# Recurrent scan: where and when a segment's softmax and its local products are worked out

## The chip, the cores and the metric

The program runs on one core of a Trainium2 chip. Its time is the device time of one execution, from start to end, in microseconds; lower is better. Its four engines that matter here are TensorE (PE), VectorE (DVE), ScalarE (ACT) and GpSimd (POOL); SyncE (SP) issues the transfers. Each engine works through its own queue in order, and queues wait for one another by semaphores.

## The reference

Two blocks of a small model over x of 16 sequences, 512 positions, 128 features. The first block (attention in two forms, a mixture of experts) is not touched. The second is an attention with memory, over segments of 32 positions, 16 heads of 64, plus a linear layer in fp8 precision of the same normalized x:

```python
def step(carry, inp):                      # for each of 16 segments, every sequence and head
    mem, z = carry
    q_s, k_s, v_s, qn_s, kn_s = inp        # q, k with rotation by position; qn, kn without
    scores = jnp.einsum('bhnd,bhmd->bhnm', q_s, k_s) * SCALE
    scores = jnp.where(mask, scores, -jnp.inf)
    sdpa = jnp.einsum('bhnm,bhmd->bhnd', jax.nn.softmax(scores, axis=-1), v_s)
    sq = elu1(qn_s)
    mem_out = (sq @ mem) / (sq @ z + 1e-06)
    out = beta * mem_out + (1.0 - beta) * sdpa
    sk = elu1(kn_s)
    prev_v = (sk @ mem) / (sk @ z)
    mem = mem + sk.T @ (v_s - prev_v)
    z = z + sk.sum(axis=2)
    return ((mem, z), out)
```

and after the scan `out @ w_out`, added to x and to the fp8 layer's result with its bias.

## The kernel before

The second block is the function `scan`. Its queues are written out by hand: `turn` has one block with a loop over s for each engine, and in step s an engine does what stands there for pair s, s-1, s-2 and so on. A "pair" p is one segment and two heads: 16 segments of 8 pairs (`PAIRS`), so `PT` = 128 pairs, one a step, and a few steps more to empty the pipeline (133 in all). All 16 sequences are worked on together: as 4 groups g (`BG`) by 4 places f (`B1`), with the 32 positions of a segment for place f on partitions 32f to 32f+31.

For pair p the work goes: TensorE projects q and k, features on partitions, 512 columns (L2031), and v (L2037), into two banks of PSUM that take turns. ScalarE makes the parts of elu (L2180, L2182, L2185), VectorE finishes sigma of q (L2241), GpSimd sigma of k (`sigma_k`, L1990). VectorE starts the rotation of q or k (`rope`, L2234, L2235), GpSimd ends it (`rotate`, L1995, L1998). TensorE makes the scores one step later (L2071 the mask, L2076), VectorE takes the row maximum (L2279) and subtracts it (L2280), ScalarE exponentiates (L2202), VectorE transposes the result in 32x32 squares (L2300), sums it (L2302) and inverts the sum (L2303). TensorE multiplies with v (`local`, L2065), on the four diagonal 32x32 places of its array and into one bank; VectorE scales that by 1-beta and by the inverse sum (L2262). The parts recalled from memory (`recall`, L2047) are divided by VectorE (L2272, L2274 for k; L2291 to L2294 for q); GpSimd takes the k part from v (L2010) and adds the q part to the output of the heads (L2023). TensorE turns that (`turn_heads`, L2088), ScalarE copies it (L2214), TensorE adds it to the output projection, which sums over eight pairs in one bank (L2095); after the eighth ScalarE copies it (L2209), TensorE turns it (L2100), VectorE adds it to y (L2315). TensorE's memory update (`update`, L2055) is added by VectorE (L2251). Beside it one of the eight steps each normalizes, quantizes and loads the next segment (L1834 to L1893), and y gets its fp8 part and h with bias (L1867, L2309).

What sets the order around the change, in one step s:

- TensorE: project q, local (s-2), values, recall k (s-2), turn keys (s-1), mask and scores (s-1), project k, recall q (s-2), output projection (s-4), turn heads (s-3), update (s-4).
- ScalarE: q features, key copy (s-1), v copy, exponential (s-1), k features, heads' copy (s-3).
- VectorE: scale local (s-2), rope q, sigma q, recalled k (s-2), maximum and subtraction (s-1), recalled q (s-2), rope k, transposition and sum (s-1), additions to memory (s-4).
- GpSimd: rotate q, sigma k, new values (s-2), rotate k, addition of recalled parts (s-2).

Of the kernel before, what the change touches and what calls it, by code (L numbers as in the profile page):

```python
# [18 lines left out]
BF16 = mybir.dt.bfloat16  # L19
# [1739 lines left out]
def scan(nc, c, V, out, nseg):  # L1759
# [4 lines left out]
    with ExitStack() as ctx:  # L1764
# [3 lines left out]
        def sem(n):  # L1768
# [22 lines left out]
        oT, yT = sb("oT", [P, 2, S]), sb("yT", [P, S])  # L1791
# [4 lines left out]
                 "sx se pt pvd old kr_s qr_s kd ud qd od up mu ott otc oproj yt_c yt ydone stored0 stored1").split()  # L1796
# [11 lines left out]
        table = lambda name, q: V[name][:, q].unsqueeze(1).broadcast_to([P, S // SEG, SEG])  # L1808

# [13 lines left out]
        def load(sp, seg, j):  # L1823
            for f in range(B1):
                sp.dma_start(ht[32 * f:32 * f + 32, j % 2], h_seg[f, bass.ds(seg, 1)].rearrange("o i g d -> (o i) g d")).then_inc(G[f"h_in{j % 2}"], 16)

# [38 lines left out]
        def add_bias(pool, j):  # L1865
            wait_h(pool, j)
            pool.tensor_tensor(hb[:, j % 2], ht[:, j % 2], V["bias"][:].unsqueeze(1).broadcast_to([P, BG, D]), ALU.add).then_inc(G["hb_d"], 1)  # L1867
# [23 lines left out]
        def take_xq(act, bank, j, n):  # L1891
            wait(act, "xqt", n)
            act.copy(xqT[:, j % 2], ps[:, bank, 0:256].bitcast(BF16)).then_inc(G["xqt_c"], 1)  # L1893

        def prepare(seg):

            with nc.Block() as block:

                @block.sync
                def _(sp):  # L1900
                    load(sp, seg, 0)

# [26 lines left out]
        STEPS = PT + 5  # L1929
        inside = lambda p: 0 <= p < PT  # L1930
        starts = range(0, PT, PAIRS)

        def turn(seg, more):
# [13 lines left out]
            for s in range(STEPS):  # L1947
# [8 lines left out]
                if s - 12 in starts:  # L1956
                    user(("y", (s - 12) // PAIRS), "ydone", (s - 12) // PAIRS + 1)
# [9 lines left out]
            with nc.Block() as block:  # L1967

                @block.sync
                def _(sp):  # L1970
                    for j in sorted(readied)[:2]:
                        load(sp, seg + j, j)
                    for j in range(PER):
                        wait(sp, "ydone", j + 1)
                        for f in range(B1):
                            sp.dma_start(o_seg[f, bass.ds(seg + j, 1)].rearrange("o i g d -> (o i) g d"), y[32 * f:32 * f + 32, j % 2]).then_inc(G[f"stored{j % 2}"], 16)
                        if j + 3 in readied:
                            wait(sp, "xnn_d", j + 1)
                            wait(sp, "hb_d", j + 1)
                            load(sp, seg + j + 3, j + 3)  # L1980
                    for k in range(2):
                        wait(sp, f"stored{k}", 64 * (PER // 2))

                @block.gpsimd
                def _(pool):
# [14 lines left out]
                    for s in range(STEPS):  # L2000
# [4 lines left out]
                        p = s - 2  # L2005
                        if inside(p):
# [3 lines left out]
                            pool.tensor_tensor(new, new, t1[:, p % 2].rearrange("p (g h) d -> p g h d", h=2), ALU.subtract).then_inc(G["ud"], 1)  # L2010
                        if s < PT:
# [3 lines left out]
                        for j in at_step(s, 3):  # L2015
                            wait(pool, "ffn_c", j - 1)
                            add_bias(pool, j)
                        p = s - 2
                        if inside(p):
                            wait(pool, "qd", p + 1)  # L2020
                            wait(pool, "old", p + 1)
                            o = ol[:, p % 4].rearrange("p g h d -> p (g h d)")
                            pool.tensor_tensor(o, o, t2[:, p % 2].rearrange("p c d -> p (c d)"), ALU.add).then_inc(G["od"], 1)  # L2023

                @block.tensor
                def _(pe):
# [14 lines left out]
                    def recall(p, which, done):  # L2041
                        for g in range(BG):
                            for hh in range(2):
                                rows = slice(64 * hh, 64 * hh + 64)
                                for f in range(B1):
                                    at_ = g * P + 32 * f
                                    ins = pe.matmul(ps[32 * f:32 * f + 32, 2 + hh, g * VE:(g + 1) * VE],  # L2047
# [412 lines left out]
```

## Time and profile before

| | |
|---|---|
| median of 3 runs | 3117.67 us (3115.82 to 3118.49) |
| profiled execution | 3123.61 us, span 3121.8 us |
| PE busy | 2667.9 us, 85% of the span |
| DVE busy | 2507.4 us, 80% |
| ACT busy | 1875.7 us, 60% |
| POOL busy | 1760.6 us, 56% |

The page gives for each engine its busy time over the span, and cuts the span in 40 slices; the scan is what comes after about 1705 us, the last 18 of them, in which TensorE is busy for nine tenths and GpSimd for eight, against two before. The shares of the whole span therefore say little of the scan, and the rows below are taken from it, unless their line says otherwise. An idle time before an instruction is put down to the engine that released it; "issue" is idle time in which the engine waited for nothing that the profile shows.

### The profile page before, as it was taken

Reading aid. Unit: us, or ns where it says so; the run is one execution under the profiler, and the core shown is the slowest. Engines: PE = TensorE matmul, PEld = TensorE weight load, DVE = VectorE, ACT = ScalarE, POOL = GpSimd, SP = SyncE. Lnnn points to the kernel's source line nnn. Section 1 sums busy time; section 2 is a strip of 40 time slices with the busy share of each in tenths; the row PEclk is TensorE's granted clock in tenths of the full one; section 3 lists DMA queues with packets and bytes.
Section 4 is the critical chain, followed back from the end, with each engine's and each line's share of the span. In section 5 each row is a group of like instructions: output and inputs, shape, how many; then the busy total and the mean of one; then the engine's idle time right before and its main releaser. Section 6 shows DMA issues by size and latency. Waiting matters only on the chain. (4 is left out here: it accounts for less than half of the span.)

```text
span 3121.8 us, 129631 instructions
## 1 busy us (share of the span) xinstructions
PE 2667.9 (85%) x53553; PEld 1513.3 (48%) x53553; DVE 2507.4 (80%) x7598; ACT 1875.7 (60%) x3797; POOL 1760.6 (56%) x1988
## 2 busy tenths in 40 slices
PE   5787999999999999872331899999999999999998
PEld 2342333333333333372230666666666666666665
DVE  4678898999999999586606888888888888888886
ACT  5785999999999999630001555555445555455543
POOL 5773222222222222240063888888888888888886
PEclk9896999999999999995655999999999999999999
DMA  4656444444444443192023000000000000000000
GB/s 127 211 199 174 94 94 94 96 101 93 90 93 95 106 94 87 33 325 60 6 41 93 4 11 11 11 11 5 11 11 11 11 11 11 11 11 4 11 8 11
DMA packets 173633, 201.58 MB, mean 65 GB/s; under 512 B 31152, under 2 KB 134512, under 8 KB 172784
## 3 DMA queue, kind: packets, MB, share of 16 engines
q1 hardware_dynamic: 170480, 191.87, 23.8%
q8 instruction: 427, 7.00, 1.0%
q0 software_dynamic: 2560, 1.35, 0.4%
q14 instruction: 166, 1.36, 0.2%
HBM read 125.10 MB, written 67.24 MB: 62 GB/s over the span
## 5 line engine op out<-in xcount | busy, mean ns | idle before, releaser
L845 ACT ACTIVATE at_pA<-at_ps 128x512 f32<-128x512 f32 x1024 | 552.2, 615 | 57.7 <-DVE at_ps L897 51.0
L906 DVE CUSTOM_DVE_ANT_0 at_junk<-at_ps,w_cmask 128x512 f32<-128x512 f32 (+3 forms) x1024 | 463.2, 485 | 102.5 <-PE at_ps L748 95.0
L897 DVE TENSOR_TENSOR at_ps<-at_ps,w_ratio 128x128 f32<-128x128 f32 (+3 forms) x1024 | 451.0, 491 | 2.1 <-PE at_ps L742 0.5
L714 POOL TENSOR_SCALAR_AFFINE_SELECT at_pB<-at_pB 128x128 f32<-128x128 f32 x256 | 74.8, 292 | 639.8 <-ACT at_pB L851 637.8
L851 ACT ACTIVATE at_pB<-at_ps 128x512 f32<-128x512 f32 (+1 forms) x768 | 379.8, 532 | 52.8 <-PE at_ps L755 47.5
L1995 POOL TENSOR_TENSOR sc_rb<-sc_rb,v_sin 128x512 f32<-128x512 f32 x256 | 326.0, 1273 | 43.1 <-DVE sc_ra L2235 42.0
L2031 PE MATMUL sc_ps<-sc_xT,v_wqkv 128*128 128x512 f32 x512 | 288.5, 646 | 4.6 <-issue 2.0
L742 PE MATMUL at_ps<-at_aq,at_ak 72*128 72x512 bf16 x1024 | 278.6, 388 | 0.4 <-DVE at_mx L906 0.2
L2194 ACT COPY sc_skN<-sc_ps 128x512 f32<-128x512 f32 x128 | 75.0, 586 | 324.7 <-PE sc_ps L2083 324.7
L1990 POOL TENSOR_TENSOR sc_sk<-sc_ee,sc_relu 128x512 f32<-128x512 f32 x128 | 165.6, 1294 | 184.9 <-ACT sc_ee L2185 184.8
L755 PE MATMUL at_ps<-at_bq,at_bk 75*128 75x512 bf16 (+3 forms) x1024 | 265.7, 302 | 1.5 <-ACT at_pB L851 0.9
L775 PE MATMUL at_ps<-at_pA,at_v 128*32 128x512 f32 x2048 | 263.0, 609 | 1.2 <-ACT at_oT L834 1.2
L748 PE MATMUL at_ps<-at_bk,at_bq 72*128 72x512 bf16 (+3 forms) x1024 | 224.6, 305 | 20.2 <-PEq L56 11.7
L2180 ACT ACTIVATE sc_ee<-sc_ps 128x512 f32<-128x512 f32 x256 | 150.2, 587 | 112.3 <-PE sc_ps L2031 111.2
L2234 DVE STREAM_SHUFFLE sc_rb<-sc_ps 128x512 f32<-128x512 f32 x256 | 189.4, 740 | 0.0
L2065 PEld LDWEIGHTS sc_ps<-v_uu,sc_pT 32*32 32x32 f32 x8192 | 125.5, 105 | 118.8 <-issue 112.2
L2235 DVE TENSOR_TENSOR sc_ra<-sc_ps,v_cos 128x512 f32<-128x512 f32 x256 | 172.2, 673 | 0.0
L1998 POOL TENSOR_TENSOR sc_kr<-sc_ra,sc_rb 128x512 f32<-128x512 f32 x128 | 162.9, 1272 | 10.0
L1998 POOL TENSOR_TENSOR sc_qr<-sc_ra,sc_rb 128x512 f32<-128x512 f32 x128 | 162.5, 1270 | 10.0
L2251 DVE TENSOR_TENSOR v_mem<-v_mem,sc_ps 128x520 f32<-128x520 f32 x256 | 161.7, 673 | 6.1 <-PE sc_ps L2055 6.0
L2185 ACT ACTIVATE sc_ee<-sc_ee 128x512 f32<-128x512 f32 x256 | 161.4, 631 | 8.1
L2023 POOL TENSOR_TENSOR sc_ol<-sc_ol,sc_t 128x512 f32<-128x512 f32 x128 | 163.0, 1274 | 5.6 <-DVE sc_t L2294 5.6
(317 smaller groups left out, 5955.9 us busy)
## 6 DMA issues: line engine op xcount, KB each, us to landing
parts_scratch<-fr_parts SPq DMA_DIRECT2D x64, 384.0 KB, 4.1
at_bk<-parts_scratch SPq DMA_DIRECT2D x192, 96.0 KB
at_ak<-parts_scratch SPq DMA_DIRECT2D x192, 96.0 KB
v_scratch<-fr_v SPq DMA_DIRECT2D x32, 352.0 KB, 4.4
at_v<-v_scratch SPq DMA_DIRECT2D x32, 352.0 KB, 3.5
at_bq<-parts_scratch SPq DMA_DIRECT2D x128, 64.0 KB
at_aq<-parts_scratch SPq DMA_DIRECT2D x128, 64.0 KB
on_scratch<-at_on SPq DMA_DIRECT2D x32, 256.0 KB, 2.2
```

The lines of the kernel that those rows point to most:

```text
L742: pe.matmul(ps[:, BANK[f"A{j}"], :], ak[slot][:, n % 4, j * P:(j + 1) * P], aq[slot][:, n % 4], start=True, stop=True).then_inc(filled, 1)
L748: ins = pe.matmul(ps[:, BANK[kind], col:col + wide], bq[slot][0:ROWS, n % 4, j * P:(j + 1) * P], bk[slot][0:ROWS, n % 4, 0:wide], start=Tr ...
L755: ins = pe.matmul(ps[:, BANK[kind], col:col + S - j * P], bk[slot][:, n % 4, j * P:(j + 1) * P], bq[slot][:, n % 4, j * P:S], start=True, ...
L775: ins = pe.matmul(ps[32 * s:32 * s + 32, PV, q0:S], v[:, b % 2, a, j, h * (HD + 1):h * (HD + 1) + 32], probs, start=(j == 0), stop=(j == N ...
L845: act.activation(pA[:, n % A_RING, j * S:(j + 1) * S], src, ACT.Exp).then_inc(exped, 1)
L851: act.activation(pB[:, n % T_RING, at:at + wide], src[:, 0:wide], ACT.Exp).then_inc(exped, 1)
L897: dve.tensor_tensor(src[:, 0:wide], src[:, 0:wide], W["ratio"][:, S - wide:S], ALU.mult).then_inc(tilted, 1)
L906: ins = dve.tensor_tensor_reduce(junk[:, P * j * (j + 1) // 2:P * (j + 1) * (j + 2) // 2], src[:, col:col + wide], W["cmask"][:, S - wide: ...
L1995: pool.tensor_tensor(by_pos(rb[:, n % 2]), by_pos(rb[:, n % 2]), table("sin", which), ALU.mult).then_inc(G["sn"], 1)
L1998: pool.tensor_tensor(rot[which][:, p % 2], ra[:, n % 2], rb[:, n % 2], ALU.add).then_inc(G["add_d"], 1)
L2031: pe.matmul(ps[:, bank_of("qk"[which], p), :], V["wqkv"][:, col:col + P], xT[:, p // PAIRS % 2], start=True, stop=True).then_inc(G["pj"], 1)
L2234: dve.stream_shuffle(rb[:, n % 2], x, [lane ^ 1 for lane in range(32)])
```

## The change

- `local` goes one step later and behind the value projection; the place in the array is the diagonal one for even groups and its neighbour (`f ^ 1`) for odd ones, over banks 6 and 7. So odd groups' outputs lie on other partitions, and the recalled q part, h with bias and y are laid out alike; h is loaded a second time for that, and the loads and stores are split in even and odd groups.
- The q side of the rotation and the mask change sign, so the scores come out negated. VectorE takes one minimum. ScalarE makes the exponentials out of PSUM, one for each head and group (eight of 128x32), with the minimum as pointer bias, scale -1 and the row sum as second output. VectorE inverts the sums, GpSimd scales the probabilities by them ahead of the key rotation, VectorE transposes them at the beginning of the next step.
- ScalarE copies the local products out of PSUM, scaled by 1-beta, in place of VectorE; VectorE adds the recalled part, in place of GpSimd.
- The output projection has the turned heads as stationary side, so it comes out with positions on partitions: one group and four pairs a step, eight such halves a segment, each added to y by VectorE. The copy and the turning after it go. The halves of a segment are worked out while the next one runs, so the loop has 138 steps.
- TensorE waits for the exponentials, not only for the subtraction, ahead of the memory update.

Cut to its core:

```diff
+        by_ch = lambda ap: ap.rearrange("p (h g) -> p g h", h=2)
+        swapped = lambda g, f: f ^ (g % 2)
+        YCOL = 256
...
+        HALVES, AFTER = 2 * BG, PAIRS + 2
+        STEPS = PT + AFTER
+        out_half = lambda s: (divmod((s - AFTER) % HALVES, 2), (s - AFTER) // HALVES) if inside(s - AFTER) else None
...
                 @block.sync
...
+                        if j + 2 in readied:
+                            wait(sp, "ffn_c", j + 1)
+                            load_hb(sp, seg + j + 2, j + 2)
+                        wait(sp, "ydone", HALVES * (j + 1))
...
                 @block.gpsimd
...
+                        p = s - 1
+                        if inside(p):
+                            wait(pool, "smd", p + 1)
+                            probs = ss[:, p % 2].rearrange("p (g h) j -> p g h j", h=2)
+                            pool.tensor_tensor(probs, probs, bc(by_ch(sm[:, p % 4]), SEG), ALU.mult).then_inc(G["nrm"], 1)
                         if s < PT:
                             rotate(2 * s + 1)
...
-                        p = s - 2
-                        if inside(p):
-                            wait(pool, "qd", p + 1)
-                            wait(pool, "old", p + 1)
-                            o = ol[:, p % 4].rearrange("p g h d -> p (g h d)")
-                            pool.tensor_tensor(o, o, t2[:, p % 2].rearrange("p c d -> p (c d)"), ALU.add).then_inc(G["od"], 1)
...
                 @block.tensor
...
-                        for g in range(BG):
-                            for hh in range(2):
+                        for hh in range(2):
+                            for g in range(BG):
                                 for f in range(B1):
-                                    ch = 2 * g + hh
-                                    ins = pe.matmul(ps[32 * f:32 * f + 32, 6, ch * DH:(ch + 1) * DH], pT[32 * f:32 * f + 32, p % 4, ch, :],
+                                    ch, to, col = 2 * g + hh, 32 * swapped(g, f), (2 * (g // 2) + hh) * DH
+                                    ins = pe.matmul(ps[to:to + 32, 6 + g % 2, col:col + DH], pT[32 * f:32 * f + 32, p % 4, ch, :],
                                                     uu[32 * f:32 * f + 32, p % PAIRS, g, hh, 0:DH], start=True, stop=True)
...
+                    def project_out(j, g, half):
+                        few = range(half * PAIRS // 2, (half + 1) * PAIRS // 2)
+                        for h in few:
+                            ins = pe.matmul(ps[:, 7, YCOL:YCOL + D], oT[:, j % 2, h, g * P:(g + 1) * P], V["wout"][:, h], start=(h == few[0]), stop=(h == few[-1]))
+                        ins.then_inc(G["oproj"], 1)
...
-                            wait(pe, "sx", min(s, PT))
+                            wait(pe, "se", min(s, PT))
...
                 @block.scalar
...
+                        p = s - 3
+                        if inside(p):
+                            wait(act, "pvd", p + 1)
+                            for hh in range(2):
+                                ins = act.activation(to[:, :, :, hh], local[:, :, :, hh], ACT.Identity, scale=V["rest"][:, col:col + 1])
+                            ins.then_inc(G["old"], 1)
...
                             wait(act, "sx", p + 1)
-                            act.activation(ss[:, p % 2], ss[:, p % 2], ACT.Exp).then_inc(G["se"], 1)
+                            for ch in range(GH):
+                                g, hh = divmod(ch, 2)
+                                n = hh * BG + g
+                                ins = act.activation(ss[:, p % 2, ch], ps[:, 4 + hh, g * SEG:(g + 1) * SEG], ACT.Exp, bias=mx[:, n:n + 1], scale=-1.0,
+                                                     accum_out=sm[:, p % 4, n:n + 1])
+                            ins.then_inc(G["se"], 1)
...
                 @block.vector
...
+                            wait(dve, "nrm", p + 1)
+                            dve.transpose(pT[:, p % 4].rearrange("p c j -> p (c j)"), ss[:, p % 2].rearrange("p c j -> p (c j)")).then_inc(G["pt"], 1)
...
-                            link(dve.tensor_reduce(head(mx[:]), scored, AX.X, ALU.max))
-                            dve.tensor_tensor(by_head(ss[:, p % 2]), scored, bc(head(mx[:]), SEG), ALU.subtract).then_inc(G["sx"], 1)
+                            wait(dve, "se", p)
+                            dve.tensor_reduce(head(mx[:]), scored, AX.X, ALU.min).then_inc(G["sx"], 1)
...
+                            wait(dve, "se", p + 1)
+                            dve.reciprocal(sm[:, p % 4], sm[:, p % 4]).then_inc(G["smd"], 1)
                         if s < PT:
                             rope(2 * s + 1)
...
+                            dve.tensor_tensor(y[:, j % 2, g], y[:, j % 2, g], ps[:, 7, YCOL:YCOL + D], ALU.add).then_inc(G["ydone"], 1)
```

## Rows read from the trace of the kernel before

**Rows 1.** Busy time by stretch: length; PE, PEld, DVE, ACT, POOL; PEclk, DMA, GB/s

```profile
2000.00:2500.00 500.00, 460.47 (x15851) 319.79 (x15849) 428.96 (x1054) 255.76 (x481) 413.94 (x332) 0.99 0.04 11
```

**Rows 2.** One line's instructions: ns min/median/max, first and last start

```profile
L2241 DVE SCALAR_TENSOR_TENSOR sc_sq<-sc_ps,sc_ee x128: 668/677/693, 1708.7 to 3084.5; 128x512 f32<-128x512 f32 x128
```

**Rows 3.** Groups by line, 1700 to 3121.8: busy us, mean ns, idle before, releasers

```profile
L2037 PE MATMUL sc_ps<-v_wqkv,sc_xT 128*128 128x128 f32 x1024 | 149.7, 289 | 1.7 <-DVE sc_ra L2235 1.7
L2065 PE MATMUL sc_ps<-v_uu,sc_pT 32*32 32x64 f32 x8192 | 147.3, 216 | 16.0 <-DVE sc_sm L2303 8.5 <-issue 5.1
L2095 PE MATMUL sc_ps<-sc_oT,v_wout 128*128 128x512 f32 x256 | 146.5, 655 | 2.5 <-issue 2.5
...
L2055 PE MATMUL sc_ps<-v_uu,sc_skN 32*64 32x65 f32 x8192 | 120.1, 231 | 24.8 <-DVE sc_t L2294 19.8 <-issue 4.2 <-DVE v_mem L2251 0.5
```

**Rows 4.** Timeline of one turn: start, length, engine, line, idle before in brackets

```profile
2331.11 0.76 PE L2076 MATMUL sc_ps<-sc_kr,sc_qr 64*32 64x32 f32 x64
...
2332.12 0.41 DVE L2279 TENSOR_REDUCE sc_mx<-sc_ps 128x8 f32<-128x256 f32 x1
...
2333.03 0.42 ACT L2202 ACTIVATE sc_ss<-sc_ss 128x256 f32<-128x256 f32 x1 [0.84 <-DVE sc_ss L2280]
2333.35 0.58 ACT L2180 ACTIVATE sc_ee<-sc_ps 128x512 f32<-128x512 f32 x1
...
2334.45 0.63 ACT L2185 ACTIVATE sc_ee<-sc_ee 128x512 f32<-128x512 f32 x1
...
2335.28 1.29 POOL L1990 TENSOR_TENSOR sc_sk<-sc_ee,sc_relu 128x512 f32<-128x512 f32 x1
...
2336.51 1.20 POOL L2010 TENSOR_TENSOR v_uu<-v_uu,sc_t 128x512 f32<-128x512 f32 x1
...
2337.65 1.29 POOL L1995 TENSOR_TENSOR sc_rb<-sc_rb,v_sin 128x512 f32<-128x512 f32 x1
...
2339.01 1.28 POOL L1998 TENSOR_TENSOR sc_kr<-sc_ra,sc_rb 128x512 f32<-128x512 f32 x1
...
2339.55 0.74 DVE L2234 STREAM_SHUFFLE sc_rb<-sc_ps 128x512 f32<-128x512 f32 x1
...
2340.99 0.28 PE L2071 MATMUL sc_ps<-v_mask,v_ident_bf 128*128 128x128 bf16 x2
...
2342.21 0.41 DVE L2279 TENSOR_REDUCE sc_mx<-sc_ps 128x8 f32<-128x256 f32 x1
```

**Rows 5.** Groups by line and form, ScalarE, whole span

```profile
L2214 ACT COPY sc_oT<-sc_ps 128x512 f32<-128x512 f32 x128 | 75.0, 586 | 78.1 <-PE sc_ps L2088 77.8
...
L1889 ACT ACTIVATE sc_xT<-sc_ps,v_b,v_g 128x512 f32<-128x512 f32 x16 | 12.4, 776 | 33.1 <-PE sc_ps L1877 33.1
...
L1043 ACT ACTIVATE tl_ex<-tl_lg 128x32 f32<-128x32 f32 x16 | 3.9, 245 | 2.7 <-DVE tl_lg L1091 2.7
```

**Rows 6.** The same view, VectorE: reading out an accumulator

```profile
L906 DVE DVE_READ_ACCUMULATOR2_ANT at_mx<- 128x1 f32 x1024 | 83.2, 81 | 0.0
```

**Rows 7.** The same view, GpSimd: a narrow addition

```profile
L707 POOL TENSOR_TENSOR at_mrow<-at_res,at_mrow 16x128 bf16<-16x128 f32 x64 | 26.8, 419 | 5.1
```

**Rows 8.** Timeline of the first scores, which waited for GpSimd

```profile
1716.37 0.28 PE L2071 MATMUL sc_ps<-v_mask,v_ident_bf 128*128 128x128 bf16 x2 [1.66 <-POOL sc_kr L1998]
...
1716.59 0.76 PE L2076 MATMUL sc_ps<-sc_kr,sc_qr 64*32 64x32 f32 x64
...
1717.38 0.42 DVE L2279 TENSOR_REDUCE sc_mx<-sc_ps 128x8 f32<-128x256 f32 x1 [2.49 <-PE sc_ps L2076]
```

**Rows 9.** Timeline of the end: last copy of heads, last store

```profile
3112.80 0.58 ACT L2214 COPY sc_oT<-sc_ps 128x512 f32<-128x512 f32 x1 [1.75 <-PE sc_ps L2088]
...
3118.24 1.77 SPq L1976 DMA_DIRECT2D out_dram<-sc_y  x4
```

**Rows 10.** Groups by line and form, VectorE: 128x128 out of PSUM

```profile
L880 DVE TENSOR_TENSOR at_on<-at_ps,at_rr 128x128 f32<-128x128 f32 x128 | 37.3, 291 | 4.4
```

**Rows 11.** Waits of SyncE's queue, 1700 to 3121: total, times, longest

```profile
SPq L1976 <- DVE sc_y L2315: 1340.1, 16, 128.9
```

More of the change, by code:

```diff
@@ L1865, in add_bias @@
         def add_bias(pool, j):
-            wait_h(pool, j)
-            pool.tensor_tensor(hb[:, j % 2], ht[:, j % 2], V["bias"][:].unsqueeze(1).broadcast_to([P, BG, D]), ALU.add).then_inc(G["hb_d"], 1)
+            wait(pool, f"hb_in{j % 2}", 128 * max(1, (j + 1) // 2))
+            pool.tensor_tensor(hb[:, j % 2], hb[:, j % 2], V["bias"][:].unsqueeze(1).broadcast_to([P, BG, D]), ALU.add).then_inc(G["hb_d"], 1)
         def round_fp8(dve, link, n):
@@ L1892, in take_xq @@
             wait(act, "xqt", n)
-            act.copy(xqT[:, j % 2], ps[:, bank, 0:256].bitcast(BF16)).then_inc(G["xqt_c"], 1)
+            place = lambda ap: ap.rearrange("p (q o a b i) -> p q o a b i", q=2, o=2, a=2, b=2)
+            to, at = place(xqT[:, j % 2]), place(ps[:, bank, 0:256].bitcast(BF16))
+            act.copy(to[:, :, 0].rearrange("p q a b i -> p q (a b i)"), at[:, :, 0].rearrange("p q a b i -> p q (a b i)"))
+            for b in range(2):
+                ins = act.copy(to[:, :, 1, :, 1 - b], at[:, :, 1, :, b])
+            ins.then_inc(G["xqt_c"], 1)
         def prepare(seg):
@@ L2136, in _ @@
                             recall(p, 0, "qr_s")
-                        p = s - 4
-                        if inside(p):
-                            project_out(p)
+                        if out_half(s):
+                            (g, half), j = out_half(s)
+                            wait(pe, "old", min(s - 2, PT))
+                            wait(pe, "otc", j * PAIRS + 4 * half + 4)
+                            wait(pe, "ydone", s - AFTER)
+                            project_out(j, g, half)
                         p = s - 3
@@ L2212, in _ @@
                             wait(act, "ott", p + 1)
-                            wait(act, "oproj", p - 1)
-                            act.copy(oT[:, p % 2], ps[:, 6, :]).then_inc(G["otc"], 1)
+                            if p // PAIRS >= 2 and p % PAIRS == 0:
+                                wait(act, "oproj", HALVES * (p // PAIRS - 1))
+                            act.copy(oT[:, p // PAIRS % 2, p % PAIRS], ps[:, 6, :]).then_inc(G["otc"], 1)
                         for j in at_step(s, 3):
@@ L2286, in _ @@
                             round_fp8(dve, link, j)
+                        p = s - 3
+                        if inside(p):
+                            wait(dve, "old", p + 1)
+                            wait(dve, "qd", p + 1)
+                            o = ol[:, p % 4].rearrange("p g h d -> p (g h d)")
+                            dve.tensor_tensor(o, o, t2[:, p % 2].rearrange("p c d -> p (c d)"), ALU.add).then_inc(G["od"], 1)
                         p = s - 2
@@ L2299, in _ @@
                             wait(dve, "se", p + 1)
[L2300 to L2303 removed]
+                            dve.reciprocal(sm[:, p % 4], sm[:, p % 4]).then_inc(G["smd"], 1)
+                        if s < PT:
+                            rope(2 * s + 1)
                         if s - 7 in starts:
```

95 lines of the change are left out of this document (36 added, 59 removed).

## The prediction

> **What bounds the kernel now.** I read the busy shares by stretch first, then the groups by line of the tail of the program (the scan), then one turn of the timeline. The change touches the scan alone, so all else of the span stays. One row of the scan recurs 128 times and gives its rhythm: first start 1708.7, last 3084.5 us, so 1375.8/127 = 10.83 us for one step [rows 2]. In a stretch inside it TensorE is busy for 460 of 500 us, VectorE 429, GpSimd 414, ScalarE 256, at a granted clock of 0.99, which is the 2.4 GHz level [rows 1]. So TensorE is the bound, at 10.83*0.92 = 9.97 us a step. The remaining 0.86 us are mostly issue gaps, and some waits for VectorE, as before the memory update [rows 3].
>
> A full engine says what a saving may bring, but not what a longer chain costs. For that I follow the ring that links one step's scores to the next step's [rows 4]. Scores of head pair s-1 end at 2331.87; the maximum starts at 2332.12, the subtraction follows, the exponential runs 2333.03 to 2333.45, ScalarE goes on to the key features at 2333.35 and ends them at 2335.08; GpSimd makes sigma_k at 2335.28, the update of the values at 2336.51, the two halves of the key rotation from 2337.65 to 2340.29; TensorE begins the next mask at 2340.99. So the ring closes with 0.70 us to spare in a turn of 10.2 us. It is hidden now, but closely. GpSimd's order is what makes it long: the key rotation, which the next scores need, stands in its queue behind sigma_k and the values' update, and sigma_k waits for the key features, which stand in ScalarE's queue behind the softmax.
>
> **The change part by part.**
>
> 1. Local products. They move behind the value projection, one step later, and alternate over two banks and eight 32x32 places in the array in place of four. Now a pass costs 147.3/128 = 1.15 us; the nearest row is the update, also 64 records with eight places, 120.1/128 = 0.94 us [rows 3]. TensorE saves about 0.21 us a step (bounds 0 and 0.3).
> The Trainium skill (TensorEngine Tiling (Array Packing), Overview) says that 32x32 places are 16 independent tiles, which would allow up to twice the rate here. The two rows differ by a fifth, not by half; its factor would save 0.57 us of TensorE, and neither changes the time if another ring sets the step.
>
> 2. Output projection. One product of 512 columns a step (146.5/128 = 1.14 us) becomes four of 128, like the value projection (149.7/128 = 1.17 us) [rows 3]: +0.03 us. The final transposes and the copy between them go: about 0.1 us a step of TensorE, by four transposes in eight steps.
>
> 3. Softmax. VectorE loses the subtraction, the row sum and the two scalings of local products, and gains the addition of recalled parts (from GpSimd) and a small addition to y. It comes out lighter; not the bound. ScalarE loses one exponential, gains two scaled copies and eight exponentials of 128x32, each with a pointer bias and a sum. Their price is what the prediction hangs on. A plain 128x32 exponential takes 0.245 us; two pointers cost 776 - 586 = 190 ns, so one 0.095 [rows 5]; neighbours overlap by 0.10 (0.42 from 2333.03, next at 2333.35) [rows 4]. That is 0.24 us from one start to the next. The sum has to be read out: no row of ScalarE shows that, VectorE's read-out takes 0.08 [rows 6]. I take 0.32 us a head, and E = 8*0.32 + 0.10 = 2.66 us. Below it may be as short as pointer and sum for nothing: 8*0.145 + 0.10 = 1.26. Above, the read-out also costs the overlap: 8*0.42 = 3.36; a whole further instruction of plain 128x32 length less its overlap gives 8*0.385 + 0.10 = 3.2, inside that. I take the middle since its terms are measured one by one.
>
> 4. Normalizing. The probabilities are now scaled by GpSimd ahead of the key rotation. 16x128 takes it 0.419 [rows 7], 128x512 1.28 [rows 4]; in between by length 256 elements take 0.70, and 0.64 from start to start. It replaces a 1.27 us addition that stood behind the rotation, outside the ring: GpSimd does less in all, and more on the ring. Bounds 0.6 and 0.8.
>
> The ring after the change, from the end of one score to the end of the next: hop 0.03 [rows 8], minimum 0.41 [rows 4] and hop 0.05, E, features 1.63 (from the end of the exponential, 2333.45, to 2335.08), hop 0.08 (estimate, as the others), sigma_k to values' update 1.23, to the rotation 1.14, normalizing 0.64, rotation 2.64 [rows 4], hop 0.06, mask and scores 0.98 when TensorE waits for them (1716.37 to 1717.35) [rows 8]. Without E the sum is 8.89; with E = 2.66 it is 11.55. Issue gaps that fall into mask and scores, and the steps that also prepare the next segment, add something; I take 0.07: 11.62 us.
>
> Does anything beside it come later? VectorE must transpose the probabilities (0.4, taken as the minimum over as many elements) ahead of the rotation of q, and then needs 2.66 us from its start (2339.55) to the minimum (2342.21) [rows 4]. By this second ring: 0.46 + E + 1.63 + 0.08 + 1.23 + 1.14 + 0.70 + 0.06 + 0.36 (start to start) + 2.66 = 8.32 + E, half a microsecond inside the first. TensorE's value projection now waits for the k rotation on VectorE, which waits for the features: it loses some tenths there, but TensorE has only about 10.4 us of work and gaps in 11.6, so it is not late for the scores. The memory update waits for the exponentials (0.5 + E = 3.2 after the scores), about when it is reached anyway. SyncE issues twice as many transfers, of half the size, for loading and storing h and y; its queue waits 1340 us in all for y [rows 11], so they are hidden. The loads of h for the bias are placed ahead of the wait for y, and only the last store shows.
>
> The end: before, the last turned heads are copied at 3112.80 and the store starts at 3118.24, 5.4 us [rows 9]. After it seven halves follow one another, each four products, a hop, an addition of 128x128 (0.29 [rows 10]) and a hop, 1.17 + 0.4 = 1.6: some 11 us, and eight stores in place of four. Together +8 us.
>
> Sum: 11.62 - 10.83 = +0.79 us, times 127 = +100, and 8: +108. The profiled execution took 3123.6 us (span 3121.8), 5.9 above the median of 3117.7. So 3231.7 against the profiled execution, or 3226 against the median.
>
> The Trainium skill (ScalarE: Activation LUTs, What ACT_TABLE_LOAD costs) gives about 280 ns + 0.833 ns an element for an ACTIVATE with a pointer bias, less 93 ns overlap. That is 307 ns for 32 elements; the rows here give 340. By its figures alone, and the read-out free, E would be 1.8 and the step 10.8, the time of before (an estimate from that page). No run here shows the read-out on ScalarE.
>
> **The rivals.** (a) The long read-out: E = 3.36, step 8.89 + 3.36 + 0.07 = 12.32, +189 + 8: 3315 us. For it speaks that a sum cannot be read before the last element; against it, that VectorE's read-out rows are so short. (b) Read-out free, pointer paid: E = 8*0.24 + 0.10 = 2.02, step 10.98, +19 + 8: 3145. (c) Nearly equal: E of about 1.8, within 6 us of now. (d) Faster: the eight exponentials cost less than 1.7 us, pointer and sum lying under the neighbour. The ring then needs under 10.6 and TensorE stays the bound: 10.83 - 0.21 (local) - 0.07 (transposes less projection) - 0.15 (waits for a VectorE that has less to do) = 10.4, 127*0.43 = -55, + 8: 3071; with E = 1.7 about 3100. It decides at E = 1.8 (ring of 10.8). For it: TensorE is the fullest engine and really does less. Against: it needs all eight starts within 0.21 us, under the 0.245 of a plain one plus pointer less overlap. (e) The eight places don't overlap, or the projection's split costs more: TensorE keeps its 1.15 us, but it has over a microsecond of slack in the forecast, so nothing moves; only in (d) would 27 us be gone.
>
> **How the numbers follow.** Forecast mechanism with E from 2.3 to 3.0 (3180 to 3270): 0.57. (a) and up to 3.5: 0.24. (b): 0.09. (c): 0.03. (d): 0.07. (e) has 0.2 inside each and shifts none but (d). Likeliest 3226. Errors of the other terms are 0.2 us a step, 25 us. The range that leaves out (c), (d), the lower part of (b) and the top of (a) is 3155 to 3325. What a measurement of this kernel can tell from no change is about 0.2%, 6 us: faster 0.07, same 0.03, slower 0.90.
>
> **What would show it.** Starts of the exponentials 0.32 us apart, and about 2.7 us from the first to the end of the eighth; sc_sq's row at 11.6 us a step; TensorE's idle time now ahead of the mask product with GpSimd's key rotation as its releaser; TensorE's busy share down to some 83%, GpSimd's about 75%, ScalarE's up to 70% or more; local products at 0.94 a pass. Wrong it is if the mask still waits for nothing (then E is short, or the ring is not closed as I read it), if TensorE waits longest ahead of value projection or update, or if the eight exponentials take less than 1.8 us.

## The result, and the profile after

The changed kernel takes 3211.03 us (median of 4 runs, 3207.32 to 3212.26), the kernel before 3117.12 in the same comparison: a ratio of 1.0303, 95% interval 1.0279 to 1.0327. It is 94 us slower, where 108 were forecast. The profiled execution took 3210.82 us, its span is 3208.4.

First the page: busy times, and the chain that ended last. That chain ran mostly over TensorE before; now it runs over GpSimd and "issue".

```profile
PE 2661.9 (83%) x54257; PEld 1561.3 (49%) x54257; DVE 2481.4 (77%) x7326; ACT 2202.7 (69%) x5989; POOL 1681.3 (52%) x1988
POOL 29%; issue 16%; PE 1%; ACT 0%; POOLq 0%; DVE 0%
```

The stretch from 2000 to 2500 us (columns as in [rows 1]), and the row that gives the rhythm (as in [rows 2]):

```profile
2000.00:2500.00 500.00, 434.65 (x15382) 319.11 (x15382) 398.76 (x912) 357.66 (x1216) 371.91 (x319) 0.97 0.05 14
```

```profile
L2268 DVE SCALAR_TENSOR_TENSOR sc_sq<-sc_ps,sc_ee x128: 669/681/694, 1707.2 to 3159.1; 128x512 f32<-128x512 f32 x128
```

The step is (3159.1 - 1707.2)/127 = 11.43 us, against 10.83. TensorE's share fell from 92 to 87% of the scan, GpSimd's from 83 to 74%, VectorE's from 86 to 80%, ScalarE's rose from 51 to 72%. No engine is full: something that passes from one to the next sets the step. The groups by line, over the scan:

```profile
L2231 ACT ACTIVATE sc_ss<-sc_ps,sc_mx 128x32 f32<-128x32 f32 x1024 | 278.4, 298 | 130.5 <-DVE sc_mx L2300 130.5
L2231 ACT ACTIVATION_READ_ACCUMULATOR sc_ss<-sc_ps,sc_mx 128x1 f32 x1024 | 221.6, 216 | 0.0
...
L2114 PE MATMUL sc_ps<-v_wout,sc_oT 128*128 128x128 f32 x1024 | 154.4, 294 | 7.5 <-issue 3.9 <-DVE sc_y L2339 2.6 <-ACT sc_ol L2212 0.9
...
L2312 DVE TENSOR_TENSOR sc_ol<-sc_ol,sc_t 128x512 f32<-128x512 f32 x128 | 141.9, 1109 | 0.5 <-ACT sc_ol L2212 0.5
...
L2085 PE MATMUL sc_ps<-v_uu,sc_pT 32*32 32x64 f32 x8192 | 110.5, 223 | 1.8 <-issue 1.8
...
L2036 POOL TENSOR_TENSOR sc_ss<-sc_ss,sc_sm 128x256 f32<-128x256 f32 x128 | 80.8, 631 | 3.0 <-DVE sc_sm L2324 3.0
...
L2091 PE MATMUL sc_ps<-v_mask,v_ident_bf 128*128 128x128 bf16 x256 | 35.3, 219 | 72.0 <-POOL sc_kr L2019 71.2
```

What to see: TensorE was idle for 72.0 us in all ahead of the mask product (L2091), 71.2 of them for GpSimd's key rotation; in the kernel before it was 3.5 us, twice in the whole scan. The exponentials take 298 ns each, and the instructions that read out their sums (ACTIVATION_READ_ACCUMULATOR) 216, as recorded, but they overlap; the timeline has to give their spacing. It is one turn of the ring, as [rows 4] were one of before:

```profile
2335.65 0.76 PE L2096 MATMUL sc_ps<-sc_kr,sc_qr 64*32 64x32 f32 x64
...
2336.45 0.42 DVE L2300 TENSOR_REDUCE sc_mx<-sc_ps 128x8 f32<-128x256 f32 x1 [0.57 <-PE sc_ps L2096]
...
2336.91 0.29 ACT L2231 ACTIVATE sc_ss<-sc_ps,sc_mx 128x32 f32<-128x32 f32 x1 [1.02 <-DVE sc_mx L2300]
2337.09 0.19 ACT L2231 ACTIVATION_READ_ACCUMULATOR sc_ss<-sc_ps,sc_mx 128x1 f32 x1
2337.19 0.28 ACT L2231 ACTIVATE sc_ss<-sc_ps,sc_mx 128x32 f32<-128x32 f32 x1
2337.36 0.20 ACT L2231 ACTIVATION_READ_ACCUMULATOR sc_ss<-sc_ps,sc_mx 128x1 f32 x1
...
2337.45 0.29 ACT L2231 ACTIVATE sc_ss<-sc_ps,sc_mx 128x32 f32<-128x32 f32 x1
...
2338.93 0.24 ACT L2231 ACTIVATION_READ_ACCUMULATOR sc_ss<-sc_ps,sc_mx 128x1 f32 x1
...
2340.18 0.63 ACT L2199 ACTIVATE sc_ee<-sc_ee 128x512 f32<-128x512 f32 x1
...
2340.89 1.28 POOL L2011 TENSOR_TENSOR sc_sk<-sc_ee,sc_relu 128x512 f32<-128x512 f32 x1 [3.00 <-ACT sc_ee L2199]
...
2342.12 1.19 POOL L2031 TENSOR_TENSOR v_uu<-v_uu,sc_t 128x512 f32<-128x512 f32 x1
...
2343.26 0.64 POOL L2036 TENSOR_TENSOR sc_ss<-sc_ss,sc_sm 128x256 f32<-128x256 f32 x1
...
2343.84 1.29 POOL L2016 TENSOR_TENSOR sc_rb<-sc_rb,v_sin 128x512 f32<-128x512 f32 x1
...
2345.21 1.27 POOL L2019 TENSOR_TENSOR sc_kr<-sc_ra,sc_rb 128x512 f32<-128x512 f32 x1
...
2346.68 0.28 PE L2091 MATMUL sc_ps<-v_mask,v_ident_bf 128*128 128x128 bf16 x2
...
2347.69 0.42 DVE L2300 TENSOR_REDUCE sc_mx<-sc_ps 128x8 f32<-128x256 f32 x1 [0.40 <-PE sc_ps L2096]
```

The scores end at 2336.41. The minimum follows, then the first exponential at 2336.91; its read-out starts at 2337.09, the next exponential at 2337.19, the one after at 2337.45, and the last read-out ends at 2339.17. So E is 2.26 us, 0.26 to 0.27 a head. The key features end at 2340.81, then GpSimd works without a break from 2340.89 to 2346.48, and the mask product starts at 2346.68. From minimum to minimum 11.24 us.

Over the whole scan the starts of the minimum lie 11.15 to 11.20 us apart in 77 of 127 turns, and nearer in only 3. Such a sharp floor is what a ring looks like. The kernel before has none: 86 of its 127 turns are shorter than that, from 9.65 us on.

Where the 86.6 us between the two spans went: 127 * 11.43 - 127 * 10.83 = +76; the scan's first row 1.5 earlier; and from the last row of L2268 to the end 49.3 us in place of 37.3, +12. The end, where eight halves of the output projection follow one another:

```profile
3198.45 1.13 PE L2114 MATMUL sc_ps<-v_wout,sc_oT 128*128 128x128 f32 x8 [0.47 <-DVE sc_y L2339]
3199.62 0.29 DVE L2339 TENSOR_TENSOR sc_y<-sc_y,sc_ps 128x128 f32<-128x128 f32 x1 [1.31 <-PE sc_ps L2114]
...
3200.05 1.13 PE L2114 MATMUL sc_ps<-v_wout,sc_oT 128*128 128x128 f32 x8 [0.47 <-DVE sc_y L2339]
...
3203.14 3.60 SPq L2001 DMA_DIRECT2D out_dram<-sc_y  x8
```

1.60 us from one half to the next, 0.47 of it TensorE waiting for an addition to y in the same bank. The eight stores add their part: from the first of them to the end of the span 5.3 us, where the four of before [rows 9] took 3.6.

### The profile page after: what moved, and what is told of

It is laid out like the page before. It is cut to its first block and busy times, and to the rows that moved or that the text cites. A ratio compares the mean times of both kernels' runs of the same rounds, so it can differ in the third digit from the quotient of the medians.

```text
span 3208.4 us, 133350 instructions
## 1 busy us (share of the span) xinstructions
PE 2661.9 (83%) x54257; PEld 1561.3 (49%) x54257; DVE 2481.4 (77%) x7326; ACT 2202.7 (69%) x5989; POOL 1681.3 (52%) x1988
## 5 line engine op out<-in xcount | busy, mean ns | idle before, releaser
L2231 ACT ACTIVATE sc_ss<-sc_ps,sc_mx 128x32 f32<-128x32 f32 x1024 | 278.4, 298 | 130.5 <-DVE sc_mx L2300 130.5
L2050 PE MATMUL sc_ps<-sc_xT,v_wqkv 128*128 128x512 f32 x512 | 309.5, 689 | 15.3 <-DVE sc_ra L2262 12.8
L2194 ACT ACTIVATE sc_ee<-sc_ps 128x512 f32<-128x512 f32 x256 | 157.2, 614 | 94.7 <-PE sc_ps L2050 94.7
L2231 ACT ACTIVATION_READ_ACCUMULATOR sc_ss<-sc_ps,sc_mx 128x1 f32 x1024 | 221.6, 216 | 0.0
L2019 POOL TENSOR_TENSOR sc_qr<-sc_ra,sc_rb 128x512 f32<-128x512 f32 x128 | 172.9, 1351 | 10.0
L2056 PEld LDWEIGHTS sc_ps<-v_wqkv,sc_xT 128*128 128x128 f32 x1024 | 135.8, 198 | 83.6 <-DVE sc_ra L2262 37.3
```

What stands on the lines that cost most here:

```text
L2019: pool.tensor_tensor(rot[which][:, p % 2], ra[:, n % 2], rb[:, n % 2], ALU.add).then_inc(G["add_d"], 1)
L2050: pe.matmul(ps[:, bank_of("qk"[which], p), :], V["wqkv"][:, col:col + P], xT[:, p // PAIRS % 2], start=True, stop=True).then_inc(G["pj"], 1)
L2231: ins = act.activation(ss[:, p % 2, ch], ps[:, 4 + hh, g * SEG:(g + 1) * SEG], ACT.Exp, bias=mx[:, n:n + 1], scale=-1.0, accum_out=sm[:, p ...
```

## The experiments

Every kernel below the changed one ran beside the kernel before again, in three groups of four, each on a chip of its own. There the kernel before took 3113, 3109 and 3113 us in the median, and single executions of it 3097 to 3128. The changed kernel was not repeated. So kernels of different groups are to be compared by their ratios, and a difference of under some 10 us between two of them is not clear of the scatter. "Step" is the spacing of sigma_q's row, as above. "Ordinary turn" and "rounding turn" are means of the spacing of the minimum, over 112 turns and over the 15 in which VectorE also rounds the next segment to fp8.

| kernel | us | ratio to before, interval | step | ordinary turn | rounding turn |
|---|---|---|---|---|---|
| before | 3117 | | 10.83 | 10.69 | 12.23 |
| changed | 3211.0 | 1.0303 (1.0279 to 1.0327) | 11.43 | 11.27 | 12.86 |
| values' update first | 3176.5 | 1.0202 (1.018 to 1.0224) | 11.14 | 10.91 | 13.14 |
| sum by VectorE | 3168.9 | 1.0177 (1.0153 to 1.0201) | 11.12 | 10.95 | 12.64 |
| four places | 3212.7 | 1.0318 (1.0299 to 1.0338) | 11.45 | 11.35 | 12.54 |
| one exponential | 3164.1 | 1.016 (1.0142 to 1.0178) | 11.05 | 10.89 | 12.69 |
| local first | 3203.8 | 1.031 (1.0278 to 1.0342) | 11.40 | 11.26 | 12.67 |
| both orders | 3163.1 | 1.0189 (1.0155 to 1.0222) | 11.03 | 10.79 | 13.07 |
| both orders, four places | 3166.9 | 1.0192 (1.016 to 1.0224) | 11.07 | 10.85 | 13.02 |
| before, eight exponentials | 3149.4 | 1.0137 (1.0104 to 1.0169) | 11.06 | 10.88 | 12.54 |
| both orders, sum by VectorE | 3154.0 | 1.014 (1.0116 to 1.0165) | 10.99 | 10.68 | 13.50 |
| both orders, one exponential | 3171.3 | 1.0179 (1.0146 to 1.0213) | 11.19 | 10.80 | 14.47 |
| both, sum, addition by GpSimd | 3175.1 | 1.0202 (1.0185 to 1.0219) | 11.10 | 10.72 | 14.16 |
| both, one, addition by GpSimd | 3177.8 | 1.0211 (1.0182 to 1.024) | 11.20 | 10.78 | 14.54 |

**GpSimd's order (e1_values_first).** The theory: the ring of the prediction sets the step. The rival: ScalarE's load, or TensorE's waits for VectorE and ScalarE, do.

```diff
+                        p = s - 3
+                        if inside(p):
+                            new = uu[:, p % PAIRS, :, :, 0:DH]
...
                         if s < PT:
                             sigma_k(s)
-                        p = s - 3
-                        if inside(p):
-                            new = uu[:, p % PAIRS, :, :, 0:DH]
...
```

> One order changed in the changed kernel: GpSimd updates the values (1.18 us) ahead of sigma_k, not behind it. Ring theory (scores, minimum, exponentials, key features, sigma_k, values' update, normalizing, key rotation, scores sets the step of 11.43 us): the update leaves the ring and falls into GpSimd's idle time before sigma_k, the ring is 11.43 - 1.14 = 10.3 us, and something else, TensorE with its gaps at about 10.5 to 10.7, takes over: 93 to 118 us less, 3093 to 3118 us. Rival (ScalarE's queue as such, or TensorE's waits for the k rotation on VectorE and for the copied local products): GpSimd's order is nothing to it, 3211 us within 6.

35 us less (31 by the ratios): GpSimd's order does matter, so the rival falls; but a third of what I expected. The floor moved from 11.17 to 10.04 us, by the 1.14 that was taken off the ring: 13 ordinary turns lie within 0.03 of it and one below. But the other 98 are longer, 10.91 on average. The chain that ended last passes another way in some turns (start, length, what; one turn of it):

```profile
2306.25 0.44 DVE sc_mx L2300
...
2307.43 1.55 ACT sc_ss L2231 x11
2308.98 0.49 ACT sc_ee L2194
2309.47 0.50 ACT sc_relu L2196
...
2310.63 0.68 DVE sc_ra L2262
...
2311.35 1.12 PE sc_ps L2050 x2
2312.48 0.89 PE sc_ps L2056 x8
2313.37 0.80 PE sc_ps L2085 x53
...
2314.57 0.48 ACT sc_ol L2212
...
2315.09 0.66 PE sc_ps L2103 x4
2315.74 0.11 PE sc_ps L2091 x2
2315.86 0.71 PE sc_ps L2096 x46
...
2316.58 0.44 DVE sc_mx L2300
```

Minimum, exponentials, key features up to the second relu, VectorE's key rotation; this frees the bank of PSUM in which TensorE puts the value projection (L2056, behind L2050); then local products (L2085), ScalarE's copy of them, which the turned keys (L2103) wait for, mask and scores. From 2306.25 to 2316.58: 10.33 us. This is what the eight exponentials, and the local products behind the value projection, make together. I had named both waits in the prediction and not added them up as a ring. It is no floor, though: 14 ordinary turns of this kernel are shorter than 10.1 us. What it costs is tried below, with TensorE's order.

**The read-out (e2_sum_vector).**

```diff
-                                ins = act.activation(ss[:, p % 2, ch], ps[:, 4 + hh, g * SEG:(g + 1) * SEG], ACT.Exp, bias=mx[:, n:n + 1], scale=-1.0,
-                                                     accum_out=sm[:, p % 4, n:n + 1])
+                                ins = act.activation(ss[:, p % 2, ch], ps[:, 4 + hh, g * SEG:(g + 1) * SEG], ACT.Exp, bias=mx[:, n:n + 1], scale=-1.0)
...
-                            dve.reciprocal(sm[:, p % 4], sm[:, p % 4]).then_inc(G["smd"], 1)
+                            s_ = sm[:, p % 4]
+                            link(dve.tensor_reduce(head(s_), by_head(ss[:, p % 2]), AX.X, ALU.add))
+                            dve.reciprocal(s_, s_).then_inc(G["smd"], 1)
```

> In the changed kernel ScalarE's eight exponentials give no sum; VectorE sums the probabilities in one reduction (0.38 us) ahead of the reciprocal. Ring theory: each read-out takes 0.09 us of ScalarE's time, 8*0.09 = 0.75 on the ring; VectorE's sum lies beside it. Step 11.43 - 0.75 = 10.7, 95 us less: about 3116 us. Rival (VectorE or TensorE sets the step): 0 to 50 us more.

ScalarE's timeline, eight exponentials in one row:

```profile
2340.62 1.53 ACT L2231 ACTIVATE sc_ss<-sc_ps,sc_mx 128x32 f32<-128x32 f32 x8 [0.82 <-DVE sc_mx L2299]
```

1.53 in place of 2.26 us: the read-outs cost 0.73, 0.09 each. 32 of 112 ordinary turns take 10.44 us, which is 11.18 less 0.74. The price and its place on the ring are as expected. The time falls by 42 us (39 by the ratios), not 95, since the turns above the floor don't follow it down.

**The eight places (e3_four_places).** `swapped = lambda g, f: f`, so the local products use the diagonal places. In this kernel the input of the fp8 layer keeps its swapped order, so that layer's part is added to the wrong sequences in odd groups; the work is the same.

> In the changed kernel the local products go back to the four diagonal places (still two banks, one step later). Ring theory: local products take 0.2 to 0.3 us more of TensorE a step, all in slack ahead of the mask product: 3211 us within 6. Rival (TensorE sets the step): 127*0.2 = 25 to 38 us more, about 3240 us. Second question: is it the eight places that shorten a pass from 1.15 to 0.86 us, or that it follows the value projection.

```profile
L2085 PE MATMUL sc_ps<-v_uu,sc_pT 32*32 32x64 f32 x8192 | 142.0, 215 | 1.7 <-issue 1.5
```

The pass takes 142.0/128 = 1.11 us, and 110.5/128 = 0.86 with eight places: it is the places, and they are worth a quarter of a microsecond of TensorE a step. The time doesn't notice: 3212.7 against 3211.0, 1.0318 against 1.0303, within the intervals.

**The softmax undone (e5_one_exp).** VectorE subtracts and sums, ScalarE makes one exponential, as in the kernel before; all the rest stays changed.

```diff
-                            for ch in range(GH):
...
+                            act.activation(ss[:, p % 2], ss[:, p % 2], ACT.Exp).then_inc(G["se"], 1)
...
+                            link(dve.tensor_reduce(head(mx[:]), scored, AX.X, ALU.min))
+                            dve.tensor_tensor(by_head(ss[:, p % 2]), bc(head(mx[:]), SEG), scored, ALU.subtract).then_inc(G["sx"], 1)
```

> In the changed kernel the softmax goes back to subtraction by VectorE, one exponential of 128x256, and sum by VectorE; all the rest stays. Ring theory: 2.26 us of exponentials become 0.46 + 0.42, the ring 11.43 - 1.38 = 10.05, so TensorE (10.5 to 10.7) or VectorE (0.8 us more work, 9.9 in all) takes over: 3095 to 3120 us, about the time of the kernel before. Rival (the rest of the change costs the time: new waits, transfers): 3180 us or more.

47 us less than the changed kernel (45 by the ratios): half of its loss, and between my range and the rival's. The other 50 us against the kernel before stay, and the ring by itself cannot be their cause: the commonest turn is 9.78 us here, 1.40 below 11.18, and 99 of the 112 ordinary turns are longer than 10 us.

**TensorE's order (e7_local_first, e8_both_first).**

```diff
-                        if s < PT:
-                            values(s)
                         p = s - 3
                         if inside(p):
...
                             local(p)
+                        if s < PT:
+                            values(s)
```

> In the changed kernel TensorE makes the local products ahead of the value projection, as before the change, and not behind it; GpSimd's order stays the long one. Two-ring theory: the first ring (through GpSimd) stands at about 11.2 us a step and is not touched, the second (exponentials, key features, k rotation on VectorE, which frees the bank of the value projection, then local products, ScalarE's copy, turned keys, scores: 10.3 us by the chain of the run with the values' update first) is cut. So little moves: 0 to 0.2 us a step, 3186 to 3211 us. Rival (the waits of TensorE for the k rotation and for the copy set the step by themselves): 0.5 us a step or more, below 3150.

> Both orders changed: GpSimd's update of the values ahead of sigma_k, and TensorE's local products ahead of the value projection. Two-ring theory: each alone leaves the other ring; together both are cut, and TensorE with its gaps is left, 10.4 to 10.7 us a step: 11.43 - 10.6 = 0.85, 127*0.85 = 105 less than the changed kernel, 3090 to 3120 us, much more than the sum of the two alone. Rival (gains add, as shares of a common cost): 35 and 0 to 25, so 3150 to 3180.

Alone it gives 7 us by time and nothing by the ratios (1.031 against 1.0303), with 77 of 112 ordinary turns still within 0.03 us of 11.18: the first ring stands, as expected. Both orders give 48 us by time and 36 by the ratios. That is near the rival's sum of the single gains, 35 + 7 by time, 31 and nothing by the ratios, so my expectation for the pair, 90 to 120 us, fell. TensorE's order, and with it the second ring, is worth little: 11.03 us a step against 11.14 with the values' update alone. The floor is the same 10.04 us (12 turns within 0.03 of it), but the mean ordinary turn is 10.79, and it was 10.69 in the kernel before. The idle time of TensorE in 2000 to 3000 us is 107 us (66 of it issue gaps), against 129 in the changed kernel and 77 (57) before.

**The places once more (e4_both_four).** The kernel above with `swapped` as the identity, and the fp8 layer's order to match.

> As the kernel with both orders changed, but with the local products on the four diagonal places. If TensorE sets the step there, the pass that is 0.2 to 0.3 us longer shows: 25 to 35 us more than with eight places. If it is still a ring, nothing, as with the changed kernel itself (3213 against 3211).

4 us more by time, 0.04 us a step and within the scatter, where a pass takes 148.6/128 - 115.6/128 = 0.26 us longer. TensorE does not set the step by itself here either.

**One part alone (e6_before_eight).** The kernel before, with its subtraction, and eight exponentials:

```diff
-                            act.activation(ss[:, p % 2], ss[:, p % 2], ACT.Exp).then_inc(G["se"], 1)
+                            for ch in range(GH):
+                                g, hh = divmod(ch, 2)
+                                n = hh * BG + g
+                                ins = act.activation(ss[:, p % 2, ch], ss[:, p % 2, ch], ACT.Exp, accum_out=sm[:, p % 4, n:n + 1])
+                            ins.then_inc(G["se"], 1)
...
-                            link(dve.tensor_reduce(head(s_), by_head(ss[:, p % 2]), AX.X, ALU.add))
```

> The kernel before with one part of the change: ScalarE makes eight exponentials with sum in place of one, after VectorE's subtraction, and VectorE's sum goes. Ring theory: E grows from 0.42 to about 2.0 us (no pointer), the ring had 0.7 to 1.3 us to spare in its 10.83, and becomes 9.5 + 1.6 = 11.1 to 11.3: 3150 to 3175 us. Rival (ScalarE at half load has room for 1.6 us more, VectorE is relieved): 3117 us or a little less.

3149.4 beside 3108.9 for the kernel before on that chip: +40 us, though VectorE has less to do and ScalarE was half idle. A floor appears: no turn is under 10.55 us, and 23 of the 112 ordinary ones are under 10.6, where 44 of before are under 10.55. So the split exponential costs through the chain it stands in, and not through ScalarE's load. The floor is lower than the 11.1 to 11.3 us that I expected; the time, by its mean turns, is just under my range. ScalarE's timeline:

```profile
2332.78 0.21 ACT L2205 ACTIVATE sc_ss<-sc_ss 128x32 f32<-128x32 f32 x1
2332.90 0.19 ACT L2205 ACTIVATION_READ_ACCUMULATOR sc_ss<-sc_ss 128x1 f32 x1
2332.99 0.21 ACT L2205 ACTIVATE sc_ss<-sc_ss 128x32 f32<-128x32 f32 x1
```

Out of SBUF and without a pointer one head takes 0.21 us, 0.12 to the read-out and 0.09 for it, so E is 1.8 and not 2.0.

**All together (e9 to e12).** Both orders, with the sum by VectorE; with one exponential; and each with the addition of the recalled part back on GpSimd, ahead of the values' update.

> Both orders changed, and the sums by VectorE: the exponentials take 1.5 us in place of 2.26. With both orders changed the fastest turns took 10.04 us but the mean was 11.03. If a ring through the exponentials still catches the gaps of TensorE (ring theory), 0.75 us more of slack in it takes 0.2 to 0.4 us a step off the mean: 3163 - 25 to 50 = 3113 to 3138. If TensorE's own queue sets the mean, 3163 within 8.

> Both orders changed, and the softmax as before the change (subtraction and sum by VectorE, one exponential): 0.9 us in place of 2.26. Ring theory: slack grows by 1.4 us, the mean step falls by 0.3 to 0.5 us to that of TensorE, 10.6 to 10.7: 3100 to 3125, level with the kernel before or just ahead of it. Rival: VectorE, with 0.8 us more to do, eats it: 3150 or more.

> As the kernel with both orders changed and the sums by VectorE, but the recalled part is added by GpSimd again, ahead of the values' update, in its idle time before sigma_k. VectorE's addition took 1.11 us on average where 0.69 was its shortest, and TensorE waited 18 us for it in 99 steps. Expected: VectorE's load falls by 1.1 us a step, 0.1 to 0.2 us a step less: 10 to 25 us below its sister. Rival: GpSimd's 1.27 us delay sigma_k and with it the ring: 0 to 60 us more.

> Both orders changed, one exponential, and the recalled part added by GpSimd ahead of the values' update: of the change only the places, the scaled copy by ScalarE, the normalizing by GpSimd and the split projection are left. If the rings are the whole cost, this one is at TensorE's own time, 10.5 to 10.7 us a step: 3090 to 3120, a little faster than the kernel before. If it stays above 3125, some part of the rest costs time too.

Only the first may have gained against both orders alone, 9 us by time and 15 by the ratios, with intervals that overlap. The other three are 17 to 24 us slower than the first, on the same chip, and so no faster than both orders alone. None came into its expected range: the rivals of the second and third held, and by the last one's own sign, 3178 us where above 3125 was to say so, some part of the rest of the change costs time too. None beats the kernel before. The turns say where, in part: with both orders and the sum by VectorE an ordinary turn takes 10.68 us, the same as before the change, but a rounding turn 13.50, where it was 12.23. With one exponential and the addition on GpSimd it is 14.54. The four instructions that round a segment on VectorE take 2.9 us from start to end before, 3.5 with both orders and the sum by VectorE, and 4.6 in that last kernel. In such a turn of that last kernel, VectorE and GpSimd:

```profile
2388.27 1.14 DVE L1624 TENSOR_SCALAR sc_mq<-sc_tq 128x512 int32<-128x512 int32 x1
...
2389.09 1.36 POOL L2035 TENSOR_TENSOR v_uu<-v_uu,sc_t 128x512 f32<-128x512 f32 x1
...
2389.45 1.29 DVE L1625 TENSOR_SCALAR sc_mq<-sc_mq 128x512 f32<-128x512 f32 x1
...
2390.52 1.35 POOL L2011 TENSOR_TENSOR sc_sk<-sc_ee,sc_relu 128x512 f32<-128x512 f32 x1
...
2390.77 1.64 DVE L1626 TENSOR_TENSOR sc_tq<-sc_tq,sc_mq 128x512 f32<-128x512 f32 x1
...
2392.44 0.69 DVE L1627 TENSOR_TENSOR sc_xq<-sc_tq,sc_mq 128x512 bf16<-128x512 f32 x1
```

Four VectorE instructions whose shortest times are 0.42, 0.43, 0.69 and 0.69 us take 4.9 us from 2388.27 to 2393.13. The first three end 0.3 to 0.5 us after a GpSimd addition does; the fourth runs while GpSimd is idle, and takes its 0.69. The Trainium skill says of this (SBUF — State Buffer, Who interferes with whom) that a VectorE instruction with two SBUF inputs contends with a GpSimd instruction that reads SBUF, and one in a two-port mode with GpSimd as such; the trace agrees for the third, which has two SBUF inputs, with 1.64 against 0.69 us. TensorE's memory update waits for VectorE 31.4 us, 16 times, in 2000 to 3000 us, against 15.6 us, 17 times, before. So where the ring was loosened, more of GpSimd's work lies beside VectorE's rounding (1.1 us of it before, 1.6 with both orders and the sum by VectorE, 3.3 in the last kernel), and some of the gain was given back there. It is not the whole of it: with the softmax undone alone (e5_one_exp) the rounding takes 2.4 us, less than before, and the rounding turn still 12.69. That it is GpSimd's place that costs, and not its amount, was not tried alone.

The balance for both orders with the sum by VectorE: ordinary turns nothing, rounding turns 15*1.27 = 19 us, the end 12, the start 3 less, 28 us in all; the spans differ by 3150.9 - 3121.8 = 29. By the medians on one chip the two kernels are 41 us apart, since the traced execution of the kernel before lay 6 us above the median beside it, and 11 above that on the last chip. So up to 0.1 us a step of the ordinary turns may be hidden in this comparison.

## Why the prediction was right

**The ring.** Right, and by its own sum: 8.89 and the measured E of 2.26 make 11.15 us, and the most frequent turns are 11.17 and 11.18. That its parts lie on it was shown by taking them off: the floor moved by 0.74 us for 0.73 of read-outs, by 1.13 for the values' update of 1.14, by both together (9.30 us, with both orders and the sum by VectorE), and by 1.40 with one exponential. And eight exponentials in the kernel before put a floor under its turns and cost it 40 us. What they did not show is that the ring is the whole loss: taking parts off gave back 33 to 57 of the 94 us by time, and 41 us or more stayed in every kernel that has the rest of the change.

**E, the term that was mis-sized.** 2.66 was forecast, 2.26 measured: 0.26 a head for 0.32. Both pieces were near, 0.17 from exponential to read-out (0.24 forecast) and 0.09 for the read-out (0.08, by VectorE's). The term was too long because I took the spacing from the recorded length of another short activation and the pointer's price at 512 columns. The long read-out (a) and the free one (b) did not come; nor did the case of no difference.

**What lies beside the ring.** I allowed 0.07 us for gaps and for the steps that prepare a segment; it is 0.26 (11.43 less 11.17). The two errors, 0.40 too much and 0.19 too little, partly cancelled, which was luck: 76 us for 100. The end cost 12 and not 8, 1.7 of it in the eight stores, which the prediction counted in without a price of their own. The medians differ by 94 us, the spans by 87; against the median the forecast of 3226 was 15 us too high.

**The others.** Normalizing is 0.63 us, 0.58 to 0.59 to the next start, for 0.64. Local products are 0.86 for 0.94. The output projection is 154.4/128 = 1.21 for 1.17. Of case (e) the price was right, in that the places move nothing here; but the eight places do overlap. TensorE is at 87% and not 83, ScalarE at 72% as said.

**What was wrong without showing.** For (d) I put TensorE's own step at 10.4 us. With both rings loosened no kernel came below a mean of 10.99, and an ordinary turn of 10.68. The forecast took 0.28 us a step off TensorE's work; at the same granted clock of 0.99 (the 2.4 GHz level) its busy time fell from 922.6/1000*10.83 = 9.99 us a step to 892.7/1000*11.03 = 9.85 with both orders changed, by 0.14. And a saving of 0.25 us on the fullest engine was worth 2 to 4 us, within the scatter, where it could be tried. So the faster case was further off than 7 in 100. What my expectations of the runs had wrong was to take the turn as whatever is longest: once the first ring was 10.04 us, ordinary turns came to 10.7 to 10.9, above either ring and above TensorE's 9.9 of work, and cutting the second ring too took only 0.11 us more off the step.

What stays open: which part of the change costs the 41 to 65 us that no loosening of the rings gave back; 12 us are at the end. And why a rounding turn takes 13.50 us with both orders and the sum by VectorE, where it took 12.23. The trace shows 0.6 us of this as longer rounding beside GpSimd's additions, but no run moved GpSimd's work out of those turns alone. Normalizing by GpSimd, the copy by ScalarE and the split projection were not undone one by one. Nor did a run change TensorE's issue gaps, 57 us in 2000 to 3000 us of the kernel before and 66 with both orders.

## What to carry to other kernels

Before work is moved to an idle engine, follow the ring that links one step to the next and add it up; here ScalarE had half its time free, and 1.4 us more on it in the kernel before cost 40 us. Splitting one instruction into eight with a pointer and a sum each costs 0.26 us apiece here. A sum that comes with the exponential is not free either: on the ring it cost 0.73 us a step, and giving it back to VectorE made the kernel some 40 us faster. A floor in the spacing of one row, the same in most turns, tells a ring from a full engine. And when a ring is cut, don't price the gain by the next shorter ring or by the busy time of the fullest engine: 1.13 us less on the floor here gave 0.30 us a step, because 98 of the 112 ordinary turns then lay above that floor.

## What the runs showed of the hardware

ScalarE's read-out of an accumulated sum is an instruction of its own; it is recorded with 0.19 to 0.25 us, and holds the next exponential up by 0.09. An exponential of 32 columns, out of PSUM with a pointer bias and a read-out, repeats every 0.26 us, out of SBUF without a pointer every 0.21. An addition of two SBUF operands of 128x512 on VectorE takes 0.68 to 1.65 us in the changed kernel (1.11 on average). 56 of the 128 take under 0.72 us; 54 take over 1.3, and each of those starts while an instruction of GpSimd is running. Twice as many stores of half the size cost 1.7 us at the end of the program. What the additional transfers cost inside the scan was not tried alone.
